# First four output tiles of a group placed behind three products of the next group in place of two

## The reference, cut to what matters

```python
attn_out = softmax((x @ Wq) @ (x @ Wk).T * scale) @ (x @ Wv) @ Wp + bp
cms_out  = gelu(attn_out @ cW1 + cb1) @ cW2 + cb2 + one_hot(code)
modifier = gelu(concat(attn_out, cms_out) @ mW1 + mb1) @ mW2 + mb2
y        = clip(x + cms_out + modifier, 0, 1)
out      = layernorm(y + gelu(y @ W_down[e] + b_down[e]) @ W_up[e] + b_up[e]) * ln_w[e] + ln_b[e]
```

## Time and profile before

| | us |
|---|---|
| median of three runs | 1136.68 |
| lowest and highest | 1136.36, 1138.86 |
| the profiled execution | 1140.68 |
| its span, first to last instruction | 1138.4 |
| PE busy in it | 1077.0 |
| mean granted clock of TensorE, as a share of full | 0.982 |

### The profile page before, as it was taken

One profiled execution on the slowest core, in us unless ns is written; L12 is line 12 of the kernel. 1 busy time (PEld: TensorE's weight loads), 2 busy tenths in 40 slices (PEclk: granted clock), 3 DMA queues, 4 the chain that ended last, 5 costly groups with the idle time before them and its releaser, 6 DMA issues.

```text
span 1138.4 us, 13134 instructions
## 1 busy us (share of the span) xinstructions
PE 1077.0 (95%) x4736; PEld 884.8 (78%) x4736; DVE 602.5 (53%) x831; ACT 458.2 (40%) x870; POOL 549.8 (48%) x561
## 2 busy tenths in 40 slices
PE   7999999787899999999988999999889999999996
PEld 6888888566678778778867888888678888888885
DVE  3634344562655555555663455554575455455567
ACT  3524345431433433433444333343523344332665
POOL 0501155640432422432577666666887666663414
PEclk9999999989999999999999999999989999999999
DMA  7301000107221221121041112222834212213733
GB/s 259 129 2 37 16 22 20 37 1 282 70 70 56 60 70 56 61 70 42 19 139 47 65 65 65 65 65 71 344 115 145 65 65 65 66 65 139 277 102 121
DMA packets 62064, 100.51 MB, mean 88 GB/s; under 512 B 5680, under 2 KB 35376, under 8 KB 61488
## 3 DMA queue, kind: packets, MB, share of 16 engines
q1 hardware_dynamic: 61424, 98.62, 25.3%
q10 hardware_dynamic: 576, 1.05, 0.2%
HBM read 77.63 MB, written 22.02 MB: 88 GB/s over the span
## 4 chain that ended last, share of the span: by engine, by line
PE 84%; DVE 7%; ACT 2%; issue 2%; SPq 2%; DMA 2%; POOL 1%; ACTq 0%; DVEq 0%
PE bank L727 28%; PE bank L728 28%; PE bank L729 28%; SPq L459 1%; DVE c_T_f L1279 1%; DVE z L1447 1%; DMA c_B_f<-cms_kept 1%; DVE x_T_lo L1293 1%; DVE stats L1441 1%; PE bank L771 1%; DVE c_T_lo L1298 1%; POOL left_c L552 1%; DMA piece_raw<-adapter_dram 0%; POOL W_lo L552 0%; ACT acc L1076 0%
## 5 line engine op out<-in xcount | busy, mean ns | idle before, releaser
L727 PE MATMUL bank<-H_hi,W_hi 128*128 128x512 f32 x512 | 201.9, 394 | 15.5 <-issue 9.3
L552 POOL TENSOR_TENSOR left_x<-rawX,left_x 128x256 fp32r<-128x256 f32 x144 | 126.5, 879 | 163.0 <-ACT left_x L957 162.7
L729 PE MATMUL bank<-H_hi,W_lo 128*128 128x512 f32 x512 | 200.9, 392 | 0.0
L728 PE MATMUL bank<-H_lo,W_hi 128*128 128x512 f32 x512 | 200.7, 392 | 0.0
L1354 DVE TENSOR_TENSOR acc<-bank,acc 128x512 f32<-128x512 f32 x224 | 151.1, 687 | 90.6 <-PE bank L729 90.2
L1337 DVE TENSOR_TENSOR u_t<-bank,s_t 128x512 f32<-128x512 f32 x64 | 44.2, 691 | 159.4 <-PE bank L729 157.3
L727 PEld LDWEIGHTS bank<-H_hi,W_hi 128*128 128x128 f32 x512 | 97.3, 190 | 38.8 <-issue 15.2
L957 ACT ACTIVATE left_x<-rawX 128x256 fp32r<-128x256 f32 x144 | 58.1, 411 | 151.2 <-DMA rawX<-mW_dram 76.8
L727 PE MATMUL bank<-x_T_hi,left_x 128*128 128x512 f32 x256 | 101.2, 395 | 12.6 <-DVE u_t L1337 11.1
L729 PEld LDWEIGHTS bank<-H_hi,W_lo 128*128 128x128 f32 x512 | 97.0, 189 | 20.7
L728 PEld LDWEIGHTS bank<-H_lo,W_hi 128*128 128x128 f32 x512 | 97.3, 190 | 20.1
(11 more groups left out here) (184 smaller groups left out, 2329.2 us busy)
## 6 DMA issues: line engine op xcount, KB each, us to landing
rawX<-mW_dram SPq DMA_DIRECT2D x16, 512.0 KB, 3.4
rawC<-mW_dram SPq DMA_DIRECT2D x16, 512.0 KB, 5.1
W_raw<-mW_dram SPq DMA_DIRECT2D x16, 512.0 KB, 3.7
xT_raw<-xT_dram SPq DMA_DIRECT2D x4, 1024.0 KB, 8.5
x_raw<-x_dram SPq DMA_DIRECT2D x4, 1024.0 KB, 6.4
rawX<-cW_dram SPq DMA_DIRECT2D x8, 512.0 KB, 3.6
W_raw<-cW_dram SPq DMA_DIRECT2D x8, 512.0 KB, 4.0
out_dram<-z SPq DMA_DIRECT2D x16, 256.0 KB, 2.0
```

Of the source, the lines that this page charges most:

```text
L552: pool.tensor_tensor(dst, src, f32(hi), ALU.subtract).then_inc(done, 1)
L727: pe.matmul(tile, sh, mh, start=first_one and n == 0, stop=False, skip_group_check=joined_group)
L728: pe.matmul(tile, sh, ml, start=False, stop=False, skip_group_check=joined_group)
L729: last = pe.matmul(tile, sl, mh, start=False, stop=last_one and n == len(terms) - 1, skip_group_check=joined_group)
```

## The change

In every group but 0 and 16, product 2 is issued ahead of `out_tiles(g - 1, 0)` in place of behind it. Nothing else on PE and nothing on the other engines is written differently; the instructions and waits are the same ones.

```diff
                 sources = [0, 1] if is_mod(g) else [0]
-                for i in (0, 1):
+                for i in (0, 1, 2):
                     product_part(g, i, sources)
                 if g > 0:
                     out_tiles(g - 1, 0)
-                for i in (2, 3, 4):
+                for i in (3, 4):
                     product_part(g, i, sources)
                 if g > 0:
                     out_tiles(g - 1, 1)
```

## The result

| | before | after |
|---|---|---|
| median of the runs compared (six each), us | 1138.93 | 1129.35 |
| lowest and highest | 1136.36, 1141.08 | 1125.85, 1130.18 |
| profiled execution | 1140.68 | 1126.75 |
| its span | 1138.4 | 1124.5 |

The ratio is 0.9911, with a 95% interval from 0.989 to 0.9931. Of 1138.93 that is 10.1 us gained, between 7.9 and 12.5. The two medians differ by 9.6. I had forecast 12.0 us and 1124.7, with a range to 1128.5, and the median after lies above it by 0.85 us and above the forecast by 4.65. Of these, 2.25 us are the starting point: the kernel before had a median of 1136.68 in the three runs shown, 1138.93 in the six of this comparison, and 1139.36 and 1140.33 in later ones (23 and 11 runs). The other 2.4 are the gain, 9.6 in place of 12.0. The profiled pair shows yet another difference, 13.9 us, and this needs explaining too.

The account below looks back on a forecast made before the run. TensorE, holding 84% of the chain, was taken as the bound. The terms 6.75 + 1.36 + 2.72 + 1.35 - 0.2 made 12.0 us gained, so 1136.68 - 12.0 = 1124.7 us, range 1122.8 to 1128.5.

Parts of the forecast that it names:

- The cause I read off: Every second group to 13: SP's adapter piece stands behind the second weights, so ACT's gelu of C21 is late.
- Term 1: Groups 5 to 13: product 2 fills five waits of 7.6 us together, 6.65 gained, with restarts 6.75.
- the moment of release: Groups 5 to 13: release of the output tiles stays 6.8 us behind the second four of the group before.
- Term 2: Group 3: product 2 takes 1.36 us out of a wait of 2.64.
- Term 3: Group 17: product 2 takes 2.72 us of the 3.18 wait for the second weights; 0.47 is left.
- Term 4: Group 17's output tiles: with 0.47 us of wait left the clock doesn't fall, 1.35 us gained (bounds 0 and 1.35).
- Term 5: Group 23: SP's fetch goes out 1.0 us earlier and delays the cms_out transfer, 0.2 us lost (bounds 0 and 1.0).
- Step 6: What costs nothing: join U3 keeps 1.8 us of slack, SP's and ACT's steps come no later, group 24 wins nothing.
- The last step: Profiled 1140.68 lies 4.0 us above the median of the runs; difference carried over, 1136.68 - 12.0 = 1124.7.

Follow-up runs that it names:

- a2: Product 2 moved in groups 1 to 15 alone, against the kernel before: ratio 0.9915, 9.7 us faster (6.4 to 13.0).
- a3: Product 2 moved in group 17 alone, against the kernel before: ratio 0.9967, 3.8 us faster (1.9 to 5.6).
- b1_swap: Kernel before, with SP fetching the second adapter piece ahead of the second weights in groups 2 to 13: ratio 0.9893, 12.2 us faster (10.0 to 14.5).
- a1_again: The changed kernel measured once more against the kernel before: ratio 0.9904, 10.9 us faster (7.6 to 14.2).
- b5_no15: The changed kernel with group 15 back in its old order; a single execution, 1128.10 us.
- before_2: The kernel before, unchanged, run for a second trace; a single execution, 1137.87 us.
- before_3: The kernel before, unchanged, run for a third trace; a single execution, 1140.92 us.
- a4_rest: Product 2 moved in all groups but 3, 5, 7, 9, 11, 13 and 17, against the kernel before: ratio 1.0013 (0.9996 to 1.003).
- b3_four: Product 3 moved as well as product 2 ahead of the first four output tiles, against the kernel before: ratio 0.9933, 7.6 us faster (5.9 to 9.5).

## Why the prediction was off, point by point

**The mechanism was right.** Product 2 fills the wait ahead of the first four output tiles. Groups 5, 7, 9, 11 and 13 have 0.07, 0.45, 0.83, 0.38 and 0.19 us left where I had said none, 0.3 to 0.4 three times, and none. The two parts alone (a2, a3) are faster by 9.7 and 3.8 us; their sum, 13.5, is above the 10.1 and 10.9 of the whole, but the interval of a2 alone is 3.3 us wide to either side. The cause I read off, the fetch order on SP, is confirmed by b1_swap.

**Term 1, groups 5 to 13: 6.75 forecast.** The stage falls from 212.36 (mean of the three traces of before) to 206.0 (mean of after, a1_again and b5_no15): 6.4. The 0.4 missing is in the moment of release, which I took as unmoved: 1.92, 1.42 and 0.89 us of wait are left in the three traces, 1.4 on average, where my sum left 1.0. In group 9 of the changed kernel ACT waits 3.46 us for the piece where it was 2.96, with SP's issues as before behind the output tiles. In a1_again it is another group, 13, with 0.75 us left. So it goes with how long the piece is under way, which differs from group to group and from trace to trace; once no slack is left, that is paid in full.

**Term 2, group 3: 1.36 forecast, mis-sized.** The row that I took it from is not typical. Five traces have the old order in group 3, on TensorE and on SP. In four of them (before_2, before_3, a3_group17, a4_rest) products 0 and 1 run at half rate, the wait ahead of the output tiles is 1.3 us and not 2.64, and 21 or 22 matmuls run at half rate, counted by their start-to-start distances; the first trace had 5 and was back at full by product 1. In the changed kernel 0.19 us of wait is left where I had said some 1.3, as product 2 fills it at half rate (products 1 and 2 take from 287.99 to 293.27), and 17 or 18 matmuls run at half rate. So the stage falls from 34.9 in those four to 32.7: 1.1 of wait, and about 0.9 of 4 or 5 fewer matmuls at half rate (0.2 each, an estimate from 0.43 - 0.227). Against the first trace it is 0.3. With all five (34.5) the gain is 1.8; I had no row that could tell.

**Term 3, group 17: 2.72 forecast.** 3.18 - 0.52 = 2.66 measured.

**Term 4, the clock in group 17: 1.35 forecast, mis-sized.** With product 2 moved, the output tiles took 5.44 to 5.58 us in all of six traces: no fall, as forecast. But without it they did so too in three of six (before_2, b1_swap, a2_first_half; 6.91, 7.19 and 7.05 in the others). The fall behind a wait of 3.02 us is no fixed part of the kernel before. Half of 1.5 us, about 0.75, is what its absence is worth on average. My reading that 2.48 us of standing still leaves the clock alone was also drawn from one place: in the same trace another wait of 2.48 us, in group 0, is followed by half rate (last section). Together with term 3, groups 16 and 17 take 54.5 us (mean of the six) against 51.2 (mean of the other six), so 3.3 in place of 4.07. With 3 us of scatter in this stage, from the half-rate stretch that follows group 16's own wait too, the difference of the means has a standard error of some 0.8 us (from the twelve values).

**Term 5, the fetch in group 23: 0.2 forecast, nothing found.** It goes out 1 us earlier as said. The transfer of cms_out, issued at 783.63, releases DVE at 793.48, 9.85 us later, where it was 806.02 - 795.94 = 10.08. In the five traces with the earlier fetch it is 9.85 to 10.49 us, mean 10.2, and in the seven without 9.90 to 11.32, mean 10.3. The Trainium skill, page "DMA: Bandwidth & Descriptors", section "Queues, rings and completion order", says that on each DMA engine descriptors are consumed in ring order. By that the later fetch would cost nothing, and these times agree; the order itself they don't show.

```profile
783.63 0.77 SPq L434 DMA_DIRECT2D c_B_f<-cms_kept  x1
...
785.79 0.46 SPq L430 DMA_DIRECT2D x_T_hi<-x_kept  x1
...
793.48 1.23 DVE L1279 TENSOR_TENSOR c_T_f<-c_T_f,c_B_f 128x1024 f32<-128x1024 f32 x1 [4.90 <-DMA c_B_f<-cms_kept]
```

**Step 6 failed**, in the words "and nothing on them comes later", said of SP's and ACT's steps. I had followed who waits for the product that moves up, and not who waits for the output tiles that move down. In group 15 ACT's conversions of cms_out do, by way of DVE's sums, and 0.65 us is lost that the sum has at nothing.

The terms as measured, 6.4 + 1.8 + 3.3 - 0.65, make 10.8 us, which lies inside both intervals. So 1.2 of the 1.9 us between 12.0 and the first measurement's 10.1 are in the stages: term 4 and step 6 are the larger part, term 1 is 0.4 too large, and term 2, 0.4 too small, hides that. Term 5's 0.2 wasn't lost. What is left, 0.7, is inside the measurement's uncertainty and stays open.

**The starting point is the step that put the time outside the range.** The last step, to carry a difference over to 1136.68, took the median of three runs as exact. They were 2.3 us below the median of the six that the change was compared with, and my range had no room for that. The same sum from 1138.93 gives 1126.9, and the range would end at 1130.8, above the measured 1129.35. The profiled pair's 13.9 us is no measure of the change either: 1.2 of it lies ahead of the first cut (270.17 - 268.96), 1.6 in the output tiles of group 16 and the wait between them (from 569.00 to 584.89 before, from 562.46 to 576.75 after: 15.89 against 14.29) and 1.8 in the stage to group 24 (221.67 against 219.91, where two other traces of the same kernel before have 220.1). Where two traces of one kernel differ as much as the pair does, the difference isn't the change's.

## What to carry to other kernels

When a step moves up in a list, another moves down: follow who waits for both. If a wait is traced to its cause, compare filling it with removing it: here exchanging two fetches on the queue, with TensorE's list as it was, was worth 12.2 us (10.0 to 14.5), no less than moving the product in 30 groups (10.1 and 10.9), and the two together, with the product only where it still helps, 15.2 (13.5 to 16.9). A stretch at half rate that one trace shows behind a wait, and a wait that one trace shows behind such a stretch, are to be priced by several traces, and a forecast of a time needs room for the median it starts from.

## What was unexpected in the hardware

The same wait doesn't always cost the same clock. Behind 3.18 us (3.02 idle) in group 17, in six traces with the same order there, TensorE's next 24 matmuls took 5.57 to 5.59 us in three and 6.91 to 7.19 in three. Behind group 16's own wait, 3.1 us idle in all twelve traces, 7 to 14 matmuls ran at half rate in eight and none in four. Behind the wait of about 6.8 us in group 3, the last matmul at half rate started 2.3 us later in one trace of the kernel before (287.62) and 12.6 later in another (297.42).

Nor does the length of the wait decide alone. In group 0, behind a wait of 2.48 us and 80 matmuls at full rate with one pause of 1.4 us among them, the start-to-start distance grows to 0.43 us within six matmuls in eleven of the twelve traces. In the kernel before:

```profile
222.54 0.50 PE L727 MATMUL bank<-x_T_hi,left_x 128*128 128x512 f32 x1 [2.48 <-DVE u_t L1337]
...
223.36 0.63 PE L727 MATMUL bank<-x_T_hi,left_x 128*128 128x512 f32 x1
223.79 0.63 PE L728 MATMUL bank<-x_T_lo,left_x 128*128 128x512 f32 x1
```

Behind 2.48 us in group 3 of the same trace and behind 2.44 in group 16 of b3_four it stayed at 0.23. From group 1 to group 31, waits of 0.2 to 1.7 us with the clock at full ahead of them were followed by no matmul at half rate.
